# Summing the state products in pairs on GpSimd before TensorE accumulates them, in a fused Mamba and attention kernel

## What is computed

```python
deltaA = jnp.exp(delta[..., None] * A)
BX = delta[..., None] * Bm[:, :, None, :] * x[..., None]
_, hs = jax.lax.associative_scan(comb, (deltaA, BX), axis=1)
y = jnp.einsum('blds,bls->bld', hs, Cm)      # the sum over the states
return y + Dp * x
```

## Time and profile before

| what | value |
|---|---|
| median of 3 runs | 4382.27 us (4371.91 to 4396.6) |
| the profiled execution, its own time | 4383.26 us |
| its span in the profile, first to last instruction | 4381.5 us |
| its mean granted TensorE clock | 0.927 |
| TensorE matmul busy | 3443.4 us (79%) |
| ScalarE busy | 2566.7 us (59%) |
| VectorE busy | 2494.5 us (57%) |
| GpSimd busy | 1723.7 us (39%) |

### The profile page before, as it was taken

One profiled execution on the slowest core, in us unless ns is written; L12 is line 12 of the kernel. 1 busy time (PEld: TensorE's weight loads), 2 busy tenths in 40 slices (PEclk: granted clock), 3 DMA queues, 4 the chain that ended last, 5 costly groups with the idle time before them and its releaser, 6 DMA issues. The chain is left out here.

```text
span 4381.5 us, 55085 instructions
## 1 busy us (share of the span) xinstructions
PE 3443.4 (79%) x16064; PEld 1847.8 (42%) x16160; DVE 2494.5 (57%) x4239; ACT 2566.7 (59%) x5827; POOL 1723.7 (39%) x1428
## 2 busy tenths in 40 slices
PE   5787888777878787887878787787787787877776
PEld 1244344444434444344443444434444444444443
DVE  5655655656565554665556656565565656656433
ACT  4455556565665655556555565656656565565554
POOL 2353442534334353343533425344243443435332
PEclk9799999999999999999999999999999999989998
DMA  2000000000000000000000000000000000000000
GB/s 79 3 1 1 5 1 6 1 1 6 1 6 1 1 6 1 6 1 1 6 1 6 1 6 1 1 6 1 6 1 1 6 1 6 1 1 3 1 3 3
DMA packets 18384, 20.52 MB, mean 5 GB/s; under 512 B 768, under 2 KB 17152, under 8 KB 17792
## 3 DMA queue, kind: packets, MB, share of 16 engines
q1 hardware_dynamic: 18048, 16.44, 1.1%
HBM read 12.24 MB, written 4.19 MB: 4 GB/s over the span
## 5 line engine op out<-in xcount | busy, mean ns | idle before, releaser
L1428 POOL TENSOR_TENSOR hc<-hst,Cs 128x512 f32<-128x512 f32 x512 | 654.5, 1278 | 1242.0 <-DVE hst L1198 1203.9
L1198 DVE TENSOR_TENSOR_SCAN hst<-dA,bank 128x512 f32<-128x512 f32 x512 | 624.8, 1220 | 323.1 <-ACT dA L893 147.8
L548 PE MATMUL bank<-W,xs 128*128 128x512 f32 x960 | 515.5, 668 | 136.6 <-DVE tmp L1339 133.0
L522 PE MATMUL bank<-hc,C 128*128 128x512 f32 x1024 | 583.8, 656 | 31.5 <-POOL hc L1428 31.5
L899 ACT COPY Cs<-bank 128x512 f32<-128x512 f32 x512 | 298.3, 583 | 307.5 <-PE bank L535 274.2
L1190 DVE TENSOR_TENSOR bank<-u,bank 128x512 f32<-128x512 f32 x512 | 351.5, 686 | 208.5 <-PE bank L535 206.5
L1487 POOL TENSOR_TENSOR oT<-tmp 128x512 f32<-128x512 f32 x256 | 324.4, 1267 | 347.5 <-DVE tmp L1339 196.4
L1502 POOL TENSOR_TENSOR Pm<-Pm,rinv 128x512 f32<-128x512 f32 x256 | 271.0, 1059 | 425.3 <-DVE rinv L1352 406.0
L1024 ACT ACTIVATE Pm<-bank,mx 128x128 f32<-128x128 f32 x1024 | 363.0, 372 | 125.5 <-DVE mx L1359 125.5
L893 ACT ACTIVATE dA<-delta,neg_a 128x512 f32<-128x512 f32 x512 | 370.9, 724 | 44.6 <-DVE hst L1198 43.6
L535 PE MATMUL bank<-parts,sel 96*128 96x512 bf16 x1024 | 338.4, 410 | 74.1 <-issue 30.2
(11 more groups left out here) (220 smaller groups left out, 5996.8 us busy)
## 6 DMA issues: line engine op xcount, KB each, us to landing
W<-wpack SPq DMA_DIRECT2D x1, 4498.0 KB, 13.8
x_tok<-x SPq DMA_DIRECT2D x16, 256.0 KB, 2.9
out<-xa SPq DMA_DIRECT2D x16, 256.0 KB, 2.2
rot<-tables SPq DMA_DIRECT2D x2, 512.0 KB, 16.6
wc_f<-taps SPq DMA_DIRECT2D x1, 1024.0 KB, 19.4
C<-cpack SPq DMA_DIRECT2D x1, 721.0 KB, 15.0
Pm<-mask SPq DMA_DIRECT2D x1, 320.0 KB, 15.3
tmp<-rowpack SPq DMA_DIRECT2D x1, 256.0 KB, 17.5
```

Source lines behind the costliest of these rows:

```text
L522: mm(y_acc[:, :], ident, hc[:, k % 2, :], start=(k == 0), stop=(k == 2 * NS - 1))\
L548: mm(b[:, :], weights, rhs, start=True, stop=True).then_inc(full(ring, job), 1)
L1198: v.tensor_tensor_scan(o, a, b, 0.0, ALU.mult, ALU.add).then_inc(sem("a_h"), 1)
L1428: g_.tensor_tensor(hc[:, k % 2, :], hst[:, k % 2, :], Cs[:, k % 2, :], ALU.mult)\
```

## The change

GpSimd writes the product of an odd state k to a half of `bx`, a tile that nothing uses during the scan, waits for it, and adds it to the product of state k-1 in `hc`. `hc` now holds two pair sums, p = 0 to 15, so the wait for the accumulation that frees a half is for the pair two before. TensorE accumulates pair p in the slot of state 2p+3, only in slots of odd states, and the last pair in the slot behind state 31. The semaphore `a_hc` still counts the 32 products; `a_pair` is new and counts the 16 sums.

```diff
-           a_dA=2 * NS, a_Cs=2 * NS, a_bx=2 * NS, a_h=2 * NS, a_hc=2 * NS, a_yacc=2 * NS,
+           a_dA=2 * NS, a_Cs=2 * NS, a_bx=2 * NS, a_h=2 * NS, a_hc=2 * NS, a_yacc=NS, a_pair=NS,
@@ TensorE, scan
-                def accumulate(k):
-                    pe.wait_ge(*step("a_hc", i, k + 1))
-                    if k == 0:
+                def accumulate(p):
+                    pe.wait_ge(*step("a_pair", i, p + 1))
+                    if p == 0:
                         pe.wait_ge(*step("a_fo", i))
-                    mm(y_acc[:, :], ident, hc[:, k % 2, :], start=(k == 0), stop=(k == 2 * NS - 1))\
+                    mm(y_acc[:, :], ident, hc[:, p % 2, :], start=(p == 0), stop=(p == NS - 1))\
                         .then_inc(sem("a_yacc"), 1)
...
-                    if k >= 2:
-                        accumulate(k - 2)
+                    if k >= 3 and k % 2:
+                        accumulate((k - 3) // 2)
                 if hi == 2 * NS:
                     yield A_END
-                    accumulate(2 * NS - 2)
-                    accumulate(2 * NS - 1)
+                    accumulate(NS - 1)
@@ GpSimd, scan
-                    if k >= 2:
-                        pool.wait_ge(*step("a_yacc", i, k - 1))
+                    p, product = k // 2, (hc if k % 2 == 0 else bx)[:, k // 2 % 2, :]
+                    if k % 2 == 0 and p >= 2:
+                        pool.wait_ge(*step("a_yacc", i, p - 1))
                     if prior:
                         pool.wait_ge(*prior[-1])
-                    g_.tensor_tensor(hc[:, k % 2, :], hst[:, k % 2, :], Cs[:, k % 2, :], ALU.mult)\
-                        .then_inc(sem("a_hc"), 1)
+                    g_.tensor_tensor(product, hst[:, k % 2, :], Cs[:, k % 2, :], ALU.mult).then_inc(sem("a_hc"), 1)
                     prior.append(step("a_hc", i, k + 1))
+                    if k % 2:
+                        pool.wait_ge(*prior[-1])
+                        g_.tensor_tensor(hc[:, p % 2, :], hc[:, p % 2, :], product, ALU.add).then_inc(sem("a_pair"), 1)
+                        prior.append(step("a_pair", i, p + 1))
```

## The result

The kernel after takes **4498.8 us** (median of 4 runs, 4493.97 to 4510.09), the kernel before on the same chip 4389.4 (4 runs): a ratio of **1.0245, 95% interval 1.0223 to 1.0267**, or 109 us more. The forecast was 4465, with a range of 4395 to 4515; the third rival, with the clock in it, had 4505. The execution in the trace took 4510.09 us (span 4508.3), 127 us more than the profiled one of before, so what follows by rows is of a run some 11 us above its median. Its mean granted clock is 0.880, against 0.927.

The account below looks back on a forecast made before the run. A ring of ScalarE and VectorE, not TensorE, was taken to pace the attention slots with a state. +4.0 us in 15 turns, +0.8 in 14 and 12 us at the start made +83 us: 4465 us, range 4395 to 4515.

Parts of the forecast that it names:

- third rival: The emptied TensorE's clock falls more often, mean 0.90 instead of 0.927, giving 4505 us; chance 0.13.
- Step 2: Behind product 17, y3 and the waiting ScalarE come later with no idle time to cover the addition: +1.42 us a turn.
- Step 5: Products 23 and 27, before the softmax scaling, delay awaited exponentials by +1.42 us each; product 25 costs 0.
- Step 9: Turn of the loop: accumulation before the branch waits one addition more, +1.42, and VectorE's 1390 loses 1.0; together +2.4 us.
- Step 3: Behind product 19, the addition shifts when line 1487 holds VectorE's 1346: -0.3 us, bounds -1.0 and +0.8.
- Step 4: Behind product 21, the delayed 1487 holds VectorE's 1346 for 0.95 us: +0.9 us, bounds 0 and 0.95.
- Step 1: Start of the turn, TensorE bound: removed accumulations give -1.62 us at state 10 and -0.86 at state 12.
- Steps 6 and 7: Products 11, 13, 15, 29 covered by GpSimd idle time, accumulations of states 16 to 30, and the last pair: 0.
- Step 8: States 3 and 4: accumulation and feed-forward matmuls move 0.9 us later, state 4's removed accumulation gives 0.86 back: 0.
- The start: First batch's scan and states 0 to 9 of the second: GpSimd becomes the bound, +0.56 us for 21 pairs, 12 us.
- TensorE as the bound: Rival: TensorE limits the kernel, so removed accumulations make it faster, 4337 us with 14 of 16 on the path; chance 0.07.
- The additions are not covered: Denies the rival that idle GpSimd time and buffering hide the additions, about 4400 us; chance 0.10.

Follow-up runs that it names:

- e4: Kernel before plus the 256 additions behind odd products, into a tile nobody reads; TensorE still accumulates 32 products; 4463.0 us, ratio 1.0168.
- e5: Kernel after with each addition but the last moved from behind the odd product to directly ahead of the next even one; 4478.6 us, ratio 1.0185.
- e10: e6 with the addition of states 4 and 5 moved from ahead of product 6 to ahead of product 7; 4398.3 us, ratio 1.0028.
- e6: e5 with pair p accumulated in the slot of state 2p+4 instead of 2p+3, the last two behind state 31; 4420.0 us, ratio 1.0053.
- e2: Kernel after with zero-weight matmuls in even slots from state 4 on except 4, 10 and 12, and ahead of the last pair; 4478.5 us, ratio 1.0196.
- e3: Kernel after without the 256 additions; TensorE accumulates only the even states' products, odd ones are left out of y; 4389.1 us, ratio 0.9999.
- e7: e6 with a zero-weight matmul in each odd slot from state 15 on; 4415.1 us, ratio 1.0048.
- e8: e3 with zero-weight matmuls in even slots from state 4 on except 4, 10 and 12, and ahead of the last accumulation; 4388.2 us, ratio 0.9992.
- e9: Kernel before with a zero-weight matmul added in each slot of states 16 to 31; 4439.4 us, ratio 1.0121.

## Why the prediction was right, and where it was not

The direction came out, and so did the main price: the additions in their places, with TensorE's order left as it was, are 74 of the 109 us (e4), the start included. The sum was 26 us too low, and the time lies nearer to the third rival's 4505 than to the forecast. One sign failed outright: TensorE's busy time was to fall by 270 to 290 us and fell by 53, or some 90 if the records that the trace of before lacks are counted in. A turn is 2.45 us longer than forecast, and this is what is left of larger misses: steps that came out some 5 us worse (states 3 and 4, 18 to 19, 31 to 0, 16 to 17, state 10) and others some 2.5 us better (products 19 and 21 above all). That these cancel by half is luck. The steps of the sum:

- **Step 2, product 17:** +1.42 forecast, +1.25 measured. **Step 5, products 23 and 27:** +1.42 each, measured 1.32 and 1.41; product 25 nothing, as said. A dependent addition starts 0.07 us behind the product in these places (2184.87 + 1.28 to 2186.22), not 0.15, so 1.35 was the better price. e5 confirms 23 and 27 by taking them away, and 17 where the clock is full.
- **Step 9, the turn:** +0.81 for 1389 (1.0 forecast) and +1.42 in step 9 to 10 (1.42 forecast), confirmed one by one by e10 and by e6. The Trainium skill, "SBUF — State Buffer", section Who interferes with whom, gave the rule of whole instructions taking turns at the shared ports. e6 and e10 agree with it, with 1.54 and 0.67 us for the same instruction with and without an addition ahead of it.
- **Step 3, product 19:** -0.3 forecast, -1.08 measured in step 19 to 20 (-1.0 was its lower bound). Both slots gained. But step 18 to 19 lost 1.30 us, which I had at nothing. This one is the clock's: of the step's 4.86 us after has 2.1 at the half clock in the mean, before none; in the two of the twelve batches in which after has none either, the step takes 3.56; and e2, with its additions in the same places and the slots filled, is at 3.56 with 0.0.
- **Step 4, product 21:** +0.9 forecast, nothing measured (21 to 22: -0.32). The price was right and the moment was not, and it was the clock that moved it. Line 1346 comes 4.94 us behind scan 21 in the 3 of 12 batches of before in which step 20 to 21 has nothing at the half clock, and 5.11 to 5.86 us in the 9 that have some 3.4; the earlier trace rows shows the latest, at 5.86. In after that step is at the full clock in all twelve, 1345 comes at 4.94, and the addition lets 1490 go 0.03 us too late to meet it. In e4 the same holds for eleven batches. In its batch 3, with 3.4 us at the half clock in step 20 to 21, 1346 comes 5.75 us behind the scan and meets line 1487 (1493 here):
```profile
841.99 2.68 POOL L1493 TENSOR_TENSOR oT<-tmp 128x512 f32<-128x512 f32 x2
842.33 0.97 DVE L1346 TENSOR_SCALAR ssq<-ssq 128x16 f32<-128x16 f32 x1
```
It takes 0.97 us for 0.17, and step 21 to 22 takes 9.61 us for 8.0. So the forecast delay exists, and that it didn't come in after is luck of the clock.
- **Step 1, state 12:** -0.86 forecast, -0.86 measured. **State 10:** -1.62 forecast, -0.99 measured, and -1.01 in e3, where there is no addition. Why 0.6 us less came back than the price at the half clock is not shown.
- **Steps 6 and 7, no cost or gain:** held for the last pair and for products 11, 13, 15 and 29 within some 0.3 us (14 to 15: +0.29). It did not hold for states 16 and 17: step 16 to 17 is 0.72 longer, and also in e3 by 0.64, both with all 6.1 us at the half clock. Nor did it for the long step from 31 to 0, which is 0.88 longer with 20.8 us at the half clock for 17.6; after's own batches take 108.2 us there with 10.2 us of it and up to 114.4 with 27.3.
- **Step 8, states 3 and 4:** 0 forecast, +1.35 measured (+2.09 and -0.74). This is the term that was mis-sized. The delay was taken as 0.9 us; the addition took 1.56 us instead of 1.27 beside VectorE's 1370, which makes it 1.1 in the step, and in over half of the turns 1.7 us of lower clock came on top.
- **The start:** 12 forecast, 12.2 measured, in part by luck. In e4, where TensorE waits for no sum, the same two stretches are only 6.7 us longer; in e2, with the slots filled, 9.4. The rest came with TensorE's waits for the sums and the lower clock, which the forecast of this term left out.

**The rivals.** TensorE as the bound is refuted by e3 at its root: the removed accumulations are worth nothing in sum. The additions are not covered (e4). The third rival, the clock, was set against the forecast as an alternative, and it is not one: it came beside it. Clock 0.88 where it assumed 0.90; e2 shows that 20 us of the loss go away when TensorE gets work in slots where that work costs little. That is a lower bound of its part in after, as the fill itself is not free. As a way to price the clock the fill did worse than the theory had it: e7, e8 and e9 gained nothing by it. What shows the clock's cost best is one step at two lengths within one kernel, as in 3 to 4 and 18 to 19 above. The Trainium skill, "TensorE: Matmul & The Clock Gate", section HAM oscillation, points the same way: gaps between bursts of matmuls bring the half rate. What it would take for the clock to fall, no run here isolates; that TensorE's busy share fell from 79% to 75% with the half-clock time up from 36.4 to 64.0 us a turn is all that the rows say.

In all: additions by place 74 us, a little of it by the clock; the other 35 are TensorE's waits for the sums and the lower clock together. The two are not split: where the waits went, less of the turn was at the half clock (e6 took both away at once, 59 us, which overlap in part with what e5 had newly made in step 14 to 15).

## What to carry to other kernels

Ahead of moving work from the fullest engine, take the work away alone, with the sum left incomplete: e3 would have said in one run that half of the accumulations are worth nothing here. An instruction put between a result and its reader costs its whole length at each place where the reader is awaited, however idle its engine is on average; the same 16 additions a batch, with the removals, cost 109 us directly behind the product and 11 (e10) when the addition, and its reader, stand where nothing waits. A time in range can hide terms that cancel, so each term is worth checking against its own step. None of the versions beat the kernel before by more than the noise.

## What the runs showed of the hardware

- **Less work at a lower clock.** e3's TensorE has 169 us less busy time, and its granted clock fell from 0.925 to 0.904 (medians) with the time the same. In this kernel three removed accumulations gave 2.6 us a turn, and steps that spent more time at the half clock took 3.0.
- **The granted clock says little of the time across kernels.** e9 has 0.931 and 4439 us, e10 0.902 and 4398. Among the runs of one kernel it does go with the time: a line through e8's ten runs, from 0.912 to 0.923, falls 3.3 us for each 0.001, through those of e6 and e10 2.7, of e3 2.0. Which of the two moves the other, these lines don't say.
- **The port is taken from both sides.** VectorE's two-input additions hold GpSimd too: product 6 took 1.59 to 1.63 us where it overlapped 1389 or 1390, an addition 1.56 behind a tensor_scalar of 0.55, against 1.27 alone.
- **The clock moves collisions.** With step 20 to 21 at the full clock line 1346 comes 4.94 us behind scan 21, with 3.4 us of that step at the half clock 5.11 to 5.86; in e4 that decides between 0.17 and 0.97 us for it.
